# Narrow products: the two terms that share weights as one matmul of 464 columns

## The reference

```
x = x + einsum('bct,bcd->bdt', x, w0[cond])                    # mixes the 64 tokens
x = x + x @ W1 + (x @ A1[i]) @ B1[i]                           # rank 16, 16 adapters
x = x + x @ W2.T + 0.5 * (x @ A2[l]) @ B2.T                    # rank 32, 3 of 5 adapters
x = x + x @ W3.T + 2 * sum_e gate_e * (x @ A3[e].T) @ B3[e].T  # rank 16, 8 experts, top 2
```

## Time and profile before

| | us |
|---|---|
| median of three runs | 523.62 |
| lowest and highest | 523.47, 523.71 |
| the profiled execution's own time | 525.11 |
| its span, first to last instruction | 523.1 |
| TensorE busy | 515.4 |
| VectorE busy | 333.1 |
| ScalarE busy | 201.1 |
| GpSimd busy | 169.2 |

### The profile page before, as it was taken

How to read it: one execution, slowest core, us unless ns; L and a number is a source line. 1 busy time by engine, 2 the same in 40 slices (tenths; PEclk the granted TensorE clock), 3 DMA queues, 4 the chain that set the end, 5 groups by cost and what they waited for, 6 DMA issues and landing times.

```text
span 523.1 us, 8849 instructions
## 1 busy us (share of the span) xinstructions
PE 515.4 (99%) x2716; PEld 449.3 (86%) x2716; DVE 333.1 (64%) x654; ACT 201.1 (38%) x349; POOL 169.2 (32%) x250
## 2 busy tenths in 40 slices
PE   7999999999999999999999999999999999999997
PEld 7999999988988888888788788888888888888885
DVE  3798797699533333399776864756647557476464
ACT  5644652345132222267344333323332333333322
POOL 2540000002102020219546434444254434553400
PEclk9999999999999999999999999999999999999999
DMA  8911310213430202040703303313233032222312
GB/s 262 375 60 27 72 40 1 80 41 122 154 116 0 81 0 81 0 166 3 241 1 117 121 12 123 104 41 113 83 115 120 37 113 85 75 84 77 125 28 80
DMA packets 29343, 46.80 MB, mean 89 GB/s; under 512 B 12020, under 2 KB 17396, under 8 KB 29188
## 3 DMA queue, kind: packets, MB, share of 16 engines
q1 hardware_dynamic: 29124, 45.85, 26.8%
q0 software_dynamic: 192, 0.59, 0.3%
HBM read 33.39 MB, written 13.04 MB: 89 GB/s over the span
## 4 chain that ended last, share of the span: by engine, by line
PE 91%; DMA 2%; POOL 1%; issue 1%; SPq 1%; DVE 1%; POOLq 1%; ACT 1%; ACTq 0%; DVEq 0%
PE bank L1869 25%; PE bank L1803 13%; PE bank L1735 11%; PE bank L1858 8%; PE bank L1777 6%; PE bank L1789 5%; PE bank L1706 4%; PE bank L1917 4%; PE bank L1925 4%; PE bank L1690 3%; PE bank L1932 2%; PE bank L1920 1%; DMA b3raw<-in_b_dram 1%; PE bank L1919 1%; DMA w2raw<-in_w_dram 1%
## 5 line engine op out<-in xcount | busy, mean ns | idle before, releaser
L1869 PE MATMUL bank<-t_hi,em_hi 128*128 128x512 f32 x168 | 57.5, 403 | 0.0
L1165 DVE TENSOR_TENSOR w1t_lo<-raw,w1t_hi 128x1024 fp32r<-128x1024 f32 x18 | 24.5, 1362 | 23.3 <-ACT w1t_hi L897 17.1
L672 POOL TENSOR_TENSOR tmp<-raw 128x512 f32<-128x512 f32 x4 | 7.2, 1794 | 97.0 <-DVE raw L1351 97.0
L1869 PEld LDWEIGHTS bank<-t_hi,em_hi 128*128 128x128 f32 x168 | 31.2, 189 | 7.2 <-DVE em_hi L1165 0.4
L1803 PE MATMUL bank<-te,em_hi 128*128 128x512 f32 x144 | 34.9, 395 | 0.0
L658 POOL CAST em_hi<-tba 128x256 fp32r x32 | 13.3, 446 | 63.6 <-PE bank L1858 60.0
L1803 PEld LDWEIGHTS bank<-te,em_hi 128*128 128x128 f32 x144 | 27.0, 188 | 6.5
L1165 DVE TENSOR_TENSOR em_hi<-tmp,em_hi 128x512 fp32r<-128x512 f32 x22 | 15.1, 686 | 21.7 <-ACT em_hi L1004 12.6
L662 POOL TENSOR_TENSOR em_lo<-tba,em_hi 128x256 fp32r<-128x256 f32 x32 | 27.4, 876 | 2.4 <-POOL em_hi L658 1.2
L1735 PE MATMUL bank<-em_hi,w2s_hi 128*128 128x384 f32 x80 | 27.0, 337 | 0.0
L1735 PE MATMUL bank<-em_lo,w2s_hi 128*128 128x384 f32 x80 | 27.0, 337 | 0.0
(11 more groups left out here) (293 smaller groups left out, 1609.0 us busy)
## 6 DMA issues: line engine op xcount, KB each, us to landing
raw<-in_x_dram SPq DMA_DIRECT2D x16, 512.0 KB, 4.0
b1s<-b1scr SPq DMA_DIRECT2D x32, 217.5 KB, 2.7
raw<-in_b1w_dram SPq DMA_DIRECT2D x10, 512.0 KB, 3.2
out_dram<-ef SPq DMA_DIRECT2D x16, 256.0 KB, 2.0
out_dram<-ost SPq DMA_DIRECT2D x16, 256.0 KB, 2.3
graw<-in_w3a3wr_dram SPq DMA_DIRECT2D x4, 768.0 KB, 11.0
b1scr<-b1stage SPq DMA_DIRECT2D x12, 256.0 KB
w2raw<-in_w_dram SPq DMA_DIRECT2D x7, 384.0 KB, 6.8
```

What stands on the lines that cost most here:

```text
L1165: V.tensor_tensor(dst, src, f32(hi), ALU.subtract).then_inc(signal, 1)
L1869: ins = nc.tensor.matmul(to[:, :], left[a][:, k0 + k, :], m_right(right, z, k), start=(name in OPENS and n == 0), stop=(n == 3 * KH - 1), ...
```

## The change

The two terms of a narrow product that have the high part of the left operand as weights become one matmul whose moving operand is the high and the low columns side by side: 2 x 232 = 464 columns, written to both halves of the bank. The third term stays a matmul of 232 columns into the first half. So each narrow product has 16 matmuls and not 24. The second half of the bank then has to be added: `xn_hi` first copies it out of the bank into XNLOW on ScalarE, `xn_lo` adds that to the first half on VectorE, and only then the split follows as before. The columns processed are the same.

In `pair_products`, `mixed` and `h1_across` stand four matmuls later for both blocks, `h1_into` three later for the first and four for the second, `h2_across` two and four later, `h2_into` two later for both, and `gated_across(b0)` two later. The first pair's order is not changed.

```
-    S = [EM[z][:, :, D:D + SC] for z in range(2)]
+    SALL = at("s_all", [P, 2, K, XC], F32R, E0)[:, :, :, D:D + SC]
+    S = [SALL[:, z, :, :] for z in range(2)]
+    XNLOW = EF[1][:, 4:8, D + SC:D + SC + SC // 4]
...
             def xn_hi(b, to):
                 act.wait_ge(s_nar, b + 1)
+                above(act, s_xna, b)
+                nc.scalar.activation(XNLOW, quarters(bank[to][:, SC:2 * SC]), ACT.Copy).then_inc(s_xnc, 1)
+                act.wait_ge(s_xna, b + 1)
...
             def xn_lo(b, to):
+                dve.wait_ge(s_xnc, b + 1)
+                V.tensor_tensor(quarters(bank[to][:, 0:SC]), quarters(bank[to][:, 0:SC]), XNLOW, ALU.add).then_inc(s_xna, 1)
                 dve.wait_ge(s_xnh, b + 1)
...
                 for k in range(K):
-                    for a, z in TERMS:
-                        ins = nc.tensor.matmul(bank[to][:, 0:SC], left(a, k), S[z][:, k, :], ...)
+                    nc.tensor.matmul(bank[to][:, 0:2 * SC].rearrange("p (z n) -> p z n", z=2), left(0, k), SALL[:, :, k, :], ...)
+                    ins = nc.tensor.matmul(bank[to][:, 0:SC], left(1, k), S[0][:, k, :], ...)
...
-                part("p3", 1, 8)
-                h2_across(b1, 1)
-                part("p3", 8, 12)
+                part("p3", 5, 12)
                 pe.wait_ge(s_add, sums + 3)
                 there("t4")
-                part("p4", 0, 2)
+                h2_across(b1, 1)
+                part("p4", 0, 4)
                 h2_into(b1, 1)
-                part("p4", 2, 12)
+                part("p4", 4, 12)
```

More of the change, by code:

```diff
@@ L356, in cond_resid_kernel @@
         s_nar = sem("s_nar")
+        s_xnc = sem("s_xnc")
+        s_xna = sem("s_xna")
         s_xnh = sem("s_xnh")
@@ L1856, in narrow @@
                 for k in range(K):
-                    for a, z in TERMS:
-                        ins = nc.tensor.matmul(bank[to][:, 0:SC], left(a, k), S[z][:, k, :], start=(k == 0 and (a, z) == TERMS[0]),
-                                               stop=(k == K - 1 and (a, z) == TERMS[-1]), skip_group_check=True)
+                    nc.tensor.matmul(bank[to][:, 0:2 * SC].rearrange("p (z n) -> p z n", z=2), left(0, k), SALL[:, :, k, :],
+                                     start=(k == 0), stop=False, skip_group_check=True)
+                    ins = nc.tensor.matmul(bank[to][:, 0:SC], left(1, k), S[0][:, k, :], start=False, stop=(k == K - 1), skip_group_check=True)
                 ins.then_inc(s_nar, 1)
@@ L2022, in there @@
                         pe.wait_ge(s_ml, SPLIT_LO[name + BACK])
-                part("p1", 0, 5)
+                part("p1", 0, 9)
                 mixed(b0, 0)
-                part("p1", 5, 11)
-                h1_across(b0, 0)
-                part("p1", 11, 12)
+                part("p1", 9, 12)
                 pe.wait_ge(s_opl, ops + 2)
                 there("t1")
-                part("p5", 0, 9)
+                part("p5", 0, 3)
+                h1_across(b0, 0)
+                part("p5", 3, 12)
                 h1_into(b0, 0, p)
-                part("p5", 9, 12)
                 pe.wait_ge(s_opl, ops + 3)
                 there("t2")
-                part("p6", 0, 4)
+                part("p6", 0, 6)
                 h2_across(b0, 0)
-                part("p6", 4, 10)
+                part("p6", 6, 12)
                 h2_into(b0, 0)
-                part("p6", 10, 12)
                 pe.wait_ge(s_opl, ops + 4)
@@ L2043, in pair_products @@
                 pe.wait_ge(s_cp, 2 * p - 1)
-                part("p2", 0, 7)
+                part("p2", 0, 11)
                 mixed(b1, 1)
-                part("p2", 7, 12)
+                part("p2", 11, 12)
                 pe.wait_ge(s_add, sums + 2)
@@ L2049, in pair_products @@
                 there("t3")
-                part("p7", 0, 5)
+                part("p7", 0, 7)
                 gated_across(b0, 0)
-                part("p7", 5, 9)
-                h1_across(b1, 1)
-                part("p7", 9, 12)
+                part("p7", 7, 12)
                 pe.wait_ge(s_opl, ops + 6)
                 part("p3", 0, 1)
+                h1_across(b1, 1)
+                part("p3", 1, 5)
                 h1_into(b1, 1, p)
-                part("p3", 1, 8)
-                h2_across(b1, 1)
-                part("p3", 8, 12)
+                part("p3", 5, 12)
                 pe.wait_ge(s_add, sums + 3)
                 there("t4")
-                part("p4", 0, 2)
+                h2_across(b1, 1)
+                part("p4", 0, 4)
                 h2_into(b1, 1)
-                part("p4", 2, 12)
+                part("p4", 4, 12)
                 if not last:
```

## The result

| | before | after |
|---|---|---|
| median of the comparison, 7 runs each | 523.62 us | 525.23 us |
| lowest and highest | 523.11, 524.29 | 524.59, 525.99 |
| ratio of the times | | 1.0031 [1.0022, 1.0040] |
| the profiled execution's own time, span | 525.11, 523.1 us | 525.23, 523.4 us |
| instructions, matmuls | 8849, 2716 | 8646, 2588 |

128 matmuls less, and 1.6 us more. The granted clock was at its full level in both. In the changed file the narrow product is at lines 1866 (464 columns) and 1868 (232), the parts at 1878, `mixed` at 1888, `gated_across` at 1915, the tiles at 1926 and following, the left operand's `left_hi` at 1008; VectorE's splits have line 1172, gh 1557.

The account below looks back on a forecast made before the run. TensorE bounds the kernel (91% of the chain). Pair 0 0.50, pair 1 0.62, pairs 2 to 5 0.60, pair 6 0, pair 7 -0.10: +1.6 us on 525.11, less 1.49 to the median, gives 525.2; range 523.3 to 527.4.

Parts of the forecast that it names:

- The saving, 13 ns a replaced pair of matmuls: Sixteen narrow products: one 464-column matmul for two of 232 saves 13 ns, 1.65 us in all.
- The upper bound of 30 ns: Narrow products: 30 ns a pair, 3.8 us in all, if a matmul's whole fixed part goes.
- the wait for h2T of pair 0: Pair 0's first narrow product: its saving is lost in the existing 0.6 us wait, h2T sitting behind a load.
- The ends of pairs 1 to 5: left_lo ends 0.19 before the last narrow product; gh then delays the tiles 0.25 us; net +0.15 a pair.
- Pair 2: Counted with pairs 2 to 5, each costing 0.15 us, 0.60 for the four.
- Pair 0: Longer split delays `mixed` by 0.25, the h1 step 0.20, third block's split 0.05: 0.50 us, from 0.1 to 0.8.
- Pair 1: Late p6 0.25, p7's late sum with the lost saving 0.12, the pair's end 0.25: 0.62 us.
- the new wait for the sum: Pair 1: p7's sum comes 0.75 us late behind the split; the 0.6 gh wait then goes; net 0.12.
- p6: Pair 1: `mixed` comes 0.92 us later, making the h1 step late for this product: 0.25, from 0 to 0.6.
- Pair 6 nothing, pair 7 -0.10: Pair 6: GpSimd's sum holds left_lo as before, cost 0; pair 7 has no left_lo and gains 0.10 us.
- Late gates of the first block: Rival: first block's gh, with 0.08 us left, meets GpSimd; 0.3 to 0.5 in six pairs, 527.6; chance 0.14.
- all waits are covered: Rival: tiles begin right behind the shorter narrow product at pair ends; full 1.65 us gained, 522.0; chance 0.09.

Follow-up runs that it names:

- e9: e5 with the narrow product's 464-column matmuls first and VectorE steps reordered in pairs 0 and 1, including p7's sum earlier; 521.22 us.
- e10: e9's order on all engines, but the narrow product of 24 matmuls of 232 columns with its old split; 522.13 us.
- e1: The kernel before with only `pair_products` in the new order, old narrow product, no copy or add; 524.53 us.
- e4: The changed kernel without the copy of the bank's second half and without the add, one product term left out; 523.66 us.
- e3: The changed kernel with VectorE's low part of the combined matrix's piece moved after the second block's gates; 524.53 us.
- e2: The changed kernel (merged narrow product, copy and add) with `pair_products` in the old order; 527.31 us.
- e6: e2 with the shorter split of e5 (no copy), old order on TensorE and VectorE; 525.32 us.
- e11: e3 with the narrow product running its eight 464-column matmuls first, waiting for left_lo only before its eight of 232; 524.01 us.
- e5: e3 with a shorter split: ScalarE rounds the first half at once without a copy, VectorE adds the second half afterwards; 523.31 us.

## Why the prediction came out right, step by step

The forecast was 525.2, the median is 525.23. The direction, the ends of the pairs and the saving came out by the mechanisms named; that the number is this close is luck. By stages the change costs 1.8 us in the trace after, against the 1.6 summed, and single terms are off by up to 0.35 with both signs.

- **The saving, 13 ns a replaced pair of matmuls.** Right: 2.58 us for the first product, and 12 ns between e9 and e10, where the loop has no wait in the list. The upper bound of 30 ns had no row, and is more than the fixed part of 13 to 17 ns that the prediction itself names. By an estimate from the Trainium skill's figure of about 2.5 ns for the fixed part ("TensorE: Matmul & The Clock Gate", section "Wait — 56ns, not 53.3ns?") 0.3 us in all would lie between those two kernels. These traces do not agree: pairs 2 to 6 alone differ by 0.9.
- **Where I took it as lost in the wait for h2T of pair 0.** Wrong, without weight: the wait comes in some traces and not in others, of kernels with the change and without it, and the trace after has none. Before's profiled execution began its first narrow product 0.72 us later than after's, and lost another 0.77 up to the product with h2T. Together that is 1.49, as much as it lay above its median; after's profiled execution is its own median.
- **The ends of pairs 1 to 5.** The mechanism was right and e1 shows it alone. One step of it was off: I had left_lo ending 0.19 before the narrow product and called that in time, while my own 0.24 from an end to the matmul behind it (used for pair 0) makes it late. From pair 2 on that 0.24 is what the trace has, so the narrow product waits too; in pair 1 it does not. Against that stands 0.07 that the new order gains in the first half of each pair, which I had not seen. The two nearly cancel: pairs 3 to 5 cost 0.18 each, forecast 0.15.
- **Pair 2** was put with them and cost 0.41. It is the loop's first turn: in VectorE's gates an idle 0.29 us stands at 342.39 that other pairs don't have, and TensorE shows its wait of 0.3 for gh there. e1, e4 and e3 don't have the idle time; what it is I did not test.
- **Pair 0.** Forecast 0.50, measured 0.59 from the mixed product on, less 0.07 for the first narrow product. The mixed product came 0.49 late and not 0.25. The rest was smaller, though a new piece came in: tile 2 loses 0.15 at the low part of its transposed gates, which stands behind a split of 2.28 us beside GpSimd (the weight load is idle for 0.31).
- **Pair 1.** Forecast 0.62, measured 0.27. I had added the new wait for the sum (0.7, seen) and the end (0.24), and taken too little for the old wait of 0.6 for gh that goes, and too much for p6 (0.25, seen 0.14). This error is -0.35 and that of pair 2 +0.26: that they cancel is chance.
- **Pair 6 nothing, pair 7 -0.10.** Measured +0.01 and +0.04. Pair 6 came right by half of its reason. I had GpSimd's sum hold left_lo as before; it held it for 0.14 and not for 0.96. Before, the hold made pair 6 longer than pairs 3 to 5 by 0.30 (34.43 against 34.13); now the order costs all four 0.18 and the hold adds 0.13 (34.44 against 34.31), which comes to nearly the same. Pair 7 is the late tile 2 told at e4.
- **The rivals.** Late gates of the first block did not happen in the changed kernel; nor did they cost in e2, and in e6 the transpose of gh comes 0.06 late, that of h1c 0.23. That all waits are covered is refuted by the trace after.

What is still open: the idle time in pair 2, why ScalarE begins 0.18 later in pair 7 with the long split, and why the narrow product of pairs 2 to 6 follows left_lo by 0.24 where that of pair 1 follows it by 0.20 without a loss.

## What to carry to other kernels

A saving on the bounding engine is worth its size only where nothing behind it is late, so count the slack of each consumer first, and take off what the profile shows between a releaser's end and the matmul behind it (0.24 us at the narrow product here). When steps are moved together, look at both sides of each: the transposes moved away from a late producer (VectorE's split) came nearer to a due consumer (the left operand), and that side cost more than this product saved. The cheap repair is to let a product start on the operand that is ready (high parts first) and to shorten the chain (round first, add the rest behind), and then to fix the few places with waits one by one.

## What the runs showed of the hardware

- A matmul that waited here cost more than the gap before it. In e3 the late narrow product began 0.30 after the matmul ahead, not 0.23, and its first 464 columns took 0.29 to the next, not 0.21; taking the wait away gave 0.13. Tile 1 in e3 lost 0.08 before and 0.10 behind its first matmul, the mixed product in e2 0.43 and 0.08.
- 464 columns in two runs of 232 take 0.214 us each in a row (eight in 376.04 - 374.33 = 1.71 us in e11), against 0.111 for one run of 232.
- VectorE's operations on SBUF beside a GpSimd operation were held up, left_lo by up to the time that one still ran: 1.23 us alone, 1.37, 1.47, 2.19 or 2.37 by how they met (in e5 it was 1.14 longer, with 1.27 of GpSimd's operation left), the gates' pair 0.48 or 1.10. The Trainium skill ("SBUF — State Buffer", section "Who interferes with whom") tells of a lock for a whole instruction, and these traces agree. A DMA set when GpSimd began, and the same chain was hit in some pairs of a trace and not in others (e4: left_lo 1.47 in pair 4, 1.23 in the rest).
